# The scan's input in the transformer block: both products and their sum on VectorE, in its drive slots

## What is computed

```python
delta   = softplus(delta_r @ W_dt.T + b_dt)
delta_b = softplus(xf @ W_xbproj.T @ W_dt.T + b_dt)          # xf: the tokens in reverse order
deltaA  = exp(delta[..., None] * A)
dBu = delta[..., None] * Bf[..., None, :] * x[..., None] \
    + delta_b[..., None] * Bb[..., None, :] * xf[..., None]
h = dA * h + du                                              # per token, 16 states n per channel
y_d = sum_n h[d, n] * c[n]
```

## Time and profile before

| | us |
|---|---|
| median of 3 runs | 7898.49 |
| lowest and highest | 7879.69 and 7908.85 |
| the profiled execution | 7906.27 |
| span of its trace | 7904.4 |

### The profile page before, as it was taken

How to read it: one execution, slowest core, us unless ns; L and a number is a source line. 1 busy time by engine, 2 the same in 40 slices (tenths; PEclk the granted TensorE clock), 3 DMA queues, 4 the chain that set the end, 5 groups by cost and what they waited for, 6 DMA issues and landing times. The chain is left out here.

```text
span 7904.4 us, 141712 instructions
## 1 busy us (share of the span) xinstructions
PE 6788.2 (86%) x45682; PEld 4620.4 (58%) x45682; DVE 4865.3 (62%) x7585; ACT 5032.1 (64%) x8721; POOL 4262.9 (54%) x1540
## 2 busy tenths in 40 slices
PE   7888789999799999799998899999999477777777
PEld 4555577777677777577776544444444255444555
DVE  7888657777467777477776333333333566777774
ACT  7888567778477777477777477777777233333332
POOL 7888457777267777177776144444444433333330
PEclk9999899999899999899999999999999687788888
DMA  2222344444444444444444411111111322333330
GB/s 84 94 98 94 129 157 158 159 158 155 162 144 159 154 156 156 153 155 158 152 159 138 140 50 45 49 50 44 50 47 41 99 67 68 69 69 69 69 68 3
DMA packets 597044, 835.29 MB, mean 106 GB/s; under 512 B 451944, under 2 KB 493032, under 8 KB 531304
## 3 DMA queue, kind: packets, MB, share of 16 engines
q1 hardware_dynamic: 596968, 834.27, 33.9%
HBM read 477.54 MB, written 356.58 MB: 106 GB/s over the span
## 5 line engine op out<-in xcount | busy, mean ns | idle before, releaser
L859 POOL TENSOR_TENSOR sb_rstd<-sb_var,sb_minus_half 128x16 f32<-128x16 f32 x1280 | 3690.0, 2900 | 2440.3 <-DVE sb_var L591 1219.3
L598 DVE TENSOR_TENSOR sb_unit<-H,sb_rstd 128x512 f32<-128x512 f32 x768 | 527.3, 687 | 517.1 <-POOL sb_rstd L859 511.7
L555 ACT ACTIVATE sb_pix<-sb_unit 128x512 f32<-128x512 f32 x768 | 827.7, 1078 | 0.0
L505 PEld LDWEIGHTS M<-sb_table,sb_pix 128*128 128x128 f32 x6144 | 712.1, 194 | 144.3 <-ACT sb_pix L555 125.1
L478 PE MATMUL H<-sb_conv_block,sb_act_in 128*128 128x128 f32 x6144 | 777.7, 280 | 0.0
L551 ACT ACTIVATE sb_act_px<-sb_unit 128x512 f32<-128x512 f32 x768 | 485.9, 633 | 451.0 <-DVE sb_unit L604 450.9
L478 PEld LDWEIGHTS H<-sb_conv_block,sb_act_in 128*128 128x128 f32 x6144 | 724.3, 194 | 38.2 <-issue 23.9
L505 PE MATMUL M<-sb_table,sb_pix 128*128 128x52 f32 x6144 | 737.0, 279 | 0.0
L591 DVE TENSOR_REDUCE sb_var<-sb_square 128x16 f32<-128x528 f32 x768 | 502.5, 696 | 236.4 <-ACT sb_square L544 236.4
L822 DVE COPY sb_act_out<-TC 128x512 f32<-128x512 f32 x256 | 177.0, 691 | 644.3 <-PE TC L672 644.3
L1812 ACT ACTIVATE blk_silu<-bank 114x260 f32<-114x260 f32 x384 | 148.7, 387 | 638.4 <-PE bank L1598 635.8
(11 more groups left out here) (273 smaller groups left out, 13588.2 us busy)
## 6 DMA issues: line engine op xcount, KB each, us to landing
act_scratch<-sb_act_out SPq DMA_DIRECT2D x256, 1024.0 KB, 3.9
sb_act_in<-act_scratch SPq DMA_DIRECT2D x256, 1024.0 KB, 5.3
spectrum_in<-sb_f_sb SPq DMA_DIRECT2D x512, 78.0 KB, 1.8
sb_x_in<-spectrum_in SPq DMA_DIRECT2D x48, 832.0 KB, 4.3
spectrum_out<-sb_y_sb SPq DMA_DIRECT2D x48, 832.0 KB, 4.6
sb_z_in<-spectrum_out SPq DMA_DIRECT2D x512, 78.0 KB, 5.1
blk_rows_b<-scan_rows SPq DMA_DIRECT2D x128, 260.0 KB, 7.2
blk_rows_bb<-scan_rows SPq DMA_DIRECT2D x128, 260.0 KB, 8.2
```

Source lines behind the costliest of these rows:

```text
L505: mm = e.matmul(M[u][:, 52 * g:52 * g + 52], pix[1 - p][:, at:at + 128], const("f1"), start=True, stop=True)
L555: e.activation(dst, unit[k % 2][:, :].rearrange("p (x c) -> p c x", c=16), gelu).then_inc(pix_ready, 1)
L598: e.tensor_tensor(rows, H[k][:, :].rearrange("p (y c) -> p y c", c=C), rstd[k][:, :].unsqueeze(2).to_broadcast([128, 16, C]), ALU.mult).th ...
L859: e.tensor_tensor(rstd[j][:, :], var[j][:, :], minus_half[:, :], ALU.pow).then_inc(rstd_ready, 1)
```

## The change

The second product and the sum go from GpSimd's list to VectorE's, directly behind the first product of the same chunk, in the same four slots. VectorE waits there for the chunk of `rows_bb` and, in the first drive slot, for `dub`. Two waits on its own semaphores stand ahead of the sum. GpSimd keeps delta, `du`, `dub` and the pair sums. The scan's wait for `input` stays where it was.

```diff
@@ VectorE, scan_slot, n in DRIVE_AT
                     e.tensor_tensor(rows, rows, du[:, :].unsqueeze(1).to_broadcast([128, NC, TOK]),
                                     ALU.mult).then_inc(sig["drive"], 1)
+                    e.wait_ge(bb_in[k], 32 * (g + 1))
+                    if k == 0:
+                        wait(e, "du", g)
+                    rows = wide(rows_bb, k).rearrange("p (n t) -> p n t", t=TOK)
+                    e.tensor_tensor(rows, rows, dub[:, :].unsqueeze(1).to_broadcast([128, NC, TOK]),
+                                    ALU.mult).then_inc(sig["drive_b"], 1)
+                    wait(e, "drive_b", g, k + 1)
+                    wait(e, "drive", g, k + 1)
+                    e.tensor_tensor(wide(rows_b, k), wide(rows_b, k), wide(rows_bb, k), ALU.add).then_inc(sig["input"], 1)
@@ GpSimd, window
-                def driven(k):
-                    e.wait_ge(bb_in[k], 32 * (gs + 1))
-                    rows = wide(rows_bb, k).rearrange("p (n t) -> p n t", t=TOK)
-                    e.tensor_tensor(rows, rows, dub[:, :].unsqueeze(1).to_broadcast([128, NC, TOK]),
-                                    ALU.mult).then_inc(sig["drive_b"], 1)
-                    wait(e, "drive_b", gs, k + 1)
-                    wait(e, "drive", gs, k + 1)
-                    e.tensor_tensor(wide(rows_b, k), wide(rows_b, k), wide(rows_bb, k), ALU.add).then_inc(sig["input"], 1)
...
-                for k in range(CHUNKS):
-                    driven(k)
```

## The result

The changed kernel takes 7945.53 us (median of 6 runs, 7934.36 to 7955.36), the one before 7895.34 beside it (6 runs): a ratio of 1.0061, 95% interval 1.0051 to 1.0071. It is slower by 50 us (40 to 56 by the interval). The profiled execution took 7949.45 us, against 7906.27 before: 43.2 more. The 29 later runs of the kernel before that were taken with the experiments lie farther apart, from 7876 to 7948 us with a median of 7901.5; against that median the changed kernel is 44 us slower.

The account below looks back on a forecast made before the run. No engine alone bounds it: TensorE paces the head and slots 0 to 5, VectorE from slot 6 to the weighting. 14 windows x 2.24, less 3, clock 0, gave +28.4 us: median 7927, range 7900 to 7966.

Parts of the forecast that it names:

- VectorE's slots 6 to 11: Packed VectorE slots: added operations cost 2.40 us per drive slot, less GpSimd delays repaid: -0.35, +2.40, -0.36, +0.35.
- The sum of a full window: Head, slot 3 and slots 6 to 11 together: +2.24 us per full window.
- rival 1: Slots 12 to 17: clock returns late after the longer weighting wait; 2.95 us more per window, 7965 us; chance 0.23.
- the collision that the prediction put at -0.1: Head: GpSimd's L2111 stretches VectorE's preparation of the scores, making TensorE wait; its removal was put at -0.1 us.
- slot 3: Added 2.40 us mostly absorbed by VectorE's waits up to slot 5; +0.3 us kept at slot 6's start.
- Rival 4: Head: its matmuls run at the fast clock level, saving up to 4 us per window; 7871 us; chance 0.04.
- clock term: Full windows: shifts of TensorE's clock changes taken as 0, bounds -1.65 to +2.95 us for each of 13 windows.
- I take -3: Window -1: without GpSimd's slower operations VectorE ends earlier; -3 us, bounds -6.8 and 0, as the next head needs `h_in`.
- Rivals 2 and 3: 2: clock returns early everywhere, 7906 us, chance 0.13; 3: GpSimd's operations not the cause, nothing repaid, 8000 us, 0.05.

Follow-up runs that it names:

- relief_only: Changed kernel without the second product and the sum on either engine; 7808.9 us, 0.9865 of the kernel before.
- dose: Kernel before plus one VectorE product on scratch tiles ahead of slot 9's scan; 7921.3 us, 1.0014 of the kernel before.
- filler_after: Changed kernel plus 12 unused TensorE matmuls ahead of its wait for the weighting; 7914.5 us, 1.0020 of the kernel before.
- full_price: Changed kernel with GpSimd also doing products and sums of the former size and order on unread scratch tiles; 8159.2 us, 1.0315 of the kernel before.
- hybrid: Changed kernel, but groups 0 and 1 (windows -1 and 0) keep the former division with both steps on GpSimd; 7952.1 us, 1.0047 of the kernel before.
- early_after: Changed kernel with drive slots 1, 3, 6, 9 instead of 3, 6, 9, 11; 7894.2 us, 0.9989 of the kernel before.
- products_first: Changed kernel with the four second products back on GpSimd, early in its list, only sums on VectorE; 7910.1 us, 1.0004 of the kernel before.
- dose3: Kernel before plus three VectorE products in slot 9, each waiting for the one before; 8006.3 us, 1.0129 of the kernel before.
- filler_before: Kernel before plus 12 unused TensorE matmuls ahead of its wait for the weighting; 7925.3 us, 1.0014 of the kernel before.

## Why the prediction was right where it was, and where not

- **VectorE's slots 6 to 11: right.** Predicted -0.35 + 2.40 - 0.36 + 0.35 = +2.04 us; measured 27.2 - 25.2 = +2.0 in the settled windows. By parts, from drive to drive to the weighting, it is -0.60, +2.20 and +0.36 for -0.35, +2.04 and +0.35. Each repaid row came out at its solo length. relief_only shows both halves of the sum on their own: against before the gain (middle 5.4 us shorter), and against after the price (5.2 for the 4.8 of two drive slots).
- **The sum of a full window: right by luck.** The mean full window grew by 2.33 us against 2.24. By the table this is head +0.78, middle -0.27, tail +1.82. With the 2.14 us that stand ahead of the memset, VectorE's part from slot 6 on is +1.87, the head up to the drive of slot 6 is 1.36 shorter (forecast: 0.2 longer) and the tail 1.82 longer (forecast: 0). The last two cancel. The tail is now always of the kind of the earlier trace rows with the late rise of the clock, so rival 1 was right about its place. Settled windows alone differ by 105.81 - 102.4 = 3.4 us; the forecast's 2.24 was nearly met because before's mean holds four long first windows.
- **The head: two terms too small, and the clock.** The first is the collision that the prediction put at -0.1. VectorE's preparation of the scores (L1931, now L1940) took 3.62 us beside GpSimd's L2111 and takes 1.44 now. TensorE paces these slots, but 0.55 us come through: the drive of slot 3 starts 37.74 us into the window, where before it was 38.3 or 40.1 in turn. The second is slot 3: from its drive to that of slot 6 it is 6.38 us for 5.80, so it costs 0.57 and not 0.3. These two cancel in the settled windows. What remains there, 0.9 us, is the clock: the drive of slot 6 now always starts 44.1 us into the window, where before it was 45.9 and 44.1 in turn. From 25 to 40 us into the window the granted clock before is 0.54 in the long windows from 6824.4 and 7029.3 and 0.77 in the short one from 6927.5, where VectorE has ended its preparation at the same 33.75 us; the changed kernel has 0.77. Rival 4 was right about this place, in part.
- **The range of the clock term was right in kind.** relief_only, dose and filler_after moved a settled window by 2.4 us more, 1.25 less and 3.4 less than the work on VectorE's path did. This is as large as everything else in the sum. Rival 1 was set behind a wait that is now longer than 6 us, but the length of the wait isn't what decides: full_price waits 7.94 us and has the early rise.
- **Windows -1 and 0: wrong, the step "I take -3".** Window -1 did end 4.7 us earlier. But the next head found its inputs missing (rows of the changed kernel; the kernel before has no wait at the first place):

```profile
6226.63 1.23 PE L1571 MATMUL bank<-blk_h_in,blk_tables 128*128 128x260 f32 x2 [1.93 <-DMA blk_h_in<-tokens]
...
6249.21 1.24 DVE L1902 TENSOR_TENSOR blk_rows_bb<-blk_rows_bb,blk_dub 128x1040 f32<-128x1040 f32 x1 [1.80 <-DMA blk_rows_bb<-scan_rows]
```

  The first L1627 of window 0 starts at 6290.81, before at 6289.70, and 0.99 of that is the later start of the block. So VectorE's saving in these windows was 0, the upper bound: the prediction had named `h_in` and not `rows_bb`, whose stores and loads also go by SyncE.
- **The clock in windows 0 and 1: missed.** The term was laid on the 13 full windows only. The projection at the end of window 0, after and before, and the first matmul of the next head after it:

```profile
6306.03 3.83 PE L1667 MATMUL bank<-blk_yt,blk_wo_head 128*128 128x260 f32 x8 [0.49 <-ACT blk_yt L1806]
6311.31 1.24 PE L1571 MATMUL bank<-blk_h,blk_tables 128*128 128x260 f32 x2 [1.45 <-DVE blk_h L1925]
```

```profile
6301.95 2.02 PE L1667 MATMUL bank<-blk_yt,blk_wo_head 128*128 128x260 f32 x8 [0.49 <-ACT blk_yt L1806]
```

  The same eight matmuls take 3.83 us instead of 2.02. Window 0 ends 4.9 us later by such rows: from its third L1627 to the end of its L1667 TensorE takes 11.9 us and not 7.2, with the same instructions. Window 1 is longer by 6.2 where 2.2 were predicted. hybrid, whose windows -1 and 0 are as before, still has +4.6 in window 1, so what window 0 did isn't the cause of most of this; its cause stays open.
- **The sum.** The block is 42.3 us longer, 13.9 more than the 28.4 of the forecast: 3 for the saving that did not come, 4.9 in window 0, 4.0 in window 1, 1.2 from the 13 full windows (13 x 0.09), 1.0 at the end (0.2 too many by rounding). The medians differ by 7 us more than the profiled pair does; the tokenizer's end moves by more than that from one execution to another, and the interval of 40 to 56 holds both.
- **Rivals 2 and 3** didn't come about. The new wait for `rows_bb` stands in windows -1 and 0 alone (5.0 us in all), as said for the full windows.

Left open: why a window settles at one length rather than another, and why the fillers' benefit in the kernel before comes only in every second window.

## What to carry to other kernels

Work moved off a slow helper engine is priced at its place: in slots where the receiving engine is packed it costs its full length less what the helper's own operations had held up. With the same instructions in earlier slots, where VectorE waits anyway, this kernel was level with the one before. Count repaid and added time by rows of one window, then treat TensorE's clock, in the head and behind its longest wait, as a term of the same size that no sum of instructions gave here, and look at what it does in the first windows too. If such a wait can't be shortened, idle matmuls in it are a cheap trial, to be made on each version anew.

## What the hardware showed that I had not expected

- Loops of unlike content settle at the same length. Windows of dose, filler_after and early_after are all 102.40 us, with middles of 24.98, 23.52 and 20.53 us. products_first has many between 101.5 and 102.5, and relief_only, after and full_price hold 95.57, 105.81 and 119.5 for eight windows or more. A change of the path of a few us can thus cost nothing in settled windows (dose: 0 for 1.25) or more than itself (relief_only: 10.2 for 7.9).
- The length of TensorE's wait doesn't tell when its clock is back. After a wait of 7.94 us (full_price) an L1598 was at 0.60 us 9.7 us after the restart, after 6.39 us (after) 14.5, and after waits of 3.0 to 3.2 us (dose3) some 9 in nine windows and 14.6 or 14.7 in four.
- TensorE's clock fell from 2.4 to 1.2 GHz while it was at work, behind a wait that had been filled with 5.4 us of matmuls (filler_before, 0.67 at 7121.67 and 1.07 at 7125.68).
- A collision moves on: in dose one product of 1.24 us pushed the next scan into a GpSimd sum (4.50 for 2.32 us) and drew a later product out of another one (1.23 for 3.29).
